# Mean of the values summed by TensorE, tokens four to a partition, GpSimd's bias rows earlier, late weights behind the first own rows

## The chip, the core and the metric

The kernel runs on one core of one Trainium2 chip. What is compared is the device time of a whole run in microseconds (us): the median of several runs of each kernel. Beside it stands one profiled execution, from which all rows below come.

## What is computed

The kernel is one layer of graph attention with a feed-forward part, with 2048 tokens, 256 features and 8 heads of 32. The adjacency `adj` is a 2048x2048 matrix of 0 and 1 with about one edge in 512, so some four edges per target row.

```python
hs = layer_norm(x, ln1_scale, ln1_bias) * mask;  ht = layer_norm(h_target, ...) * mask
q = (ht @ Wq + bq) / sqrt(32);  k = hs @ Wk + bk;  v = hs @ Wv + bv
logits = where(adj != 0, q . k, -1e30)            # per head
ctx = softmax(logits) @ v                         # a row without an edge gets the mean of v
ht = layer_norm(ht + ctx @ Wo + bo, ln2_scale, ln2_bias)
out = _layernorm(x + ht + gelu(ht @ W1) @ W2)
```

A target row with no edge has all logits at -1e30, so its softmax is flat and its context is the mean of all 2048 value rows. This mean is what the change computes in another way.

## The kernel before, in words

The kernel has two stages and a fallback path for dense graphs that these inputs do not take.

**Stage 1, the first 80 us.** The adjacency (16.8 MB of int32) is read in 16 tiles of 128 target rows (L559, `load_adj`). ScalarE turns each into a bf16 tile (`find_edges`, L1228). TensorE packs four rows at a time into integer keys (`make_keys`, L894 and L897), and VectorE picks the eight largest keys of each 128 columns (`pick_bank`, L1520), splits them into source number and bits (`split_keys`, L1526 to L1533), and lists each row's sources (`list_edges`, L1541 to L1547). This is done in four quarters. Interleaved with it, in an order written out by hand for every engine, the source tokens `x` are loaded in four chunks of 512 (`load_x`, L554), normed (VectorE `unit_stats` L1503 to L1509, GpSimd `rsqrt1` L665, ScalarE `normalise` L1211), turned (TensorE L871, ScalarE `copy_turned` L1219), projected to keys and values in 16 tiles (`project`, L883), and scaled by the node mask and biased by VectorE (`add_bias`, L1513) into `kv_out`. SyncE saves `kv_out` two tiles at a time to `kv_scratch` in DRAM (`save_kv`, L564), and copies `h_target` and `x` side by side into `tab_scratch` (L592). All these DMAs and all loads by SyncE share one hardware queue, q1; those that ScalarE issues are on q10, and GpSimd's gathers are on q0.

The values of all 16 tiles are added up by GpSimd (`add_v`, L679 and L681) into `v_total`, behind which TensorE makes the mean with one matmul over the partitions (`project_mean`, L907), ScalarE copies it out and saves it as row 0 of `kv_scratch` (L1269, L1271). GpSimd also makes three bf16 parts of the query and output biases (L737 to L747), after `add_v(1)` and behind the second quarter's split (`wait_listing(1)`). The node mask is loaded as 16 rows of 128 (L571), turned by TensorE (L915) and copied out by VectorE (L1558), and once more, per target, in the middle of the adjacency (L585).

At the end of stage 1 the rows are sorted by their number of edges. VectorE and TensorE compute every row's place (L1604 to L1658); `places` (L1656) is what the gathers need.

**Stage 2.** For each of 16 tiles of sorted rows GpSimd gathers the row's own tokens from `tab_scratch` (L765, "own rows") and, one edge slot at a time, keys and values from `kv_scratch` (L775). Before the first own gather it waits for `rows_copied`, before the first edge gather for all `kv_saved` and `mean_saved`. VectorE takes statistics (L1785), scores and weighs (L1689, L1691, L1730, L1736), ScalarE norms and applies gelu, TensorE projects (L976, L986), adds the attention's output (`project_out`, L995 to L1001, whose first call waits for all late weights), and runs the two feed-forward matmuls (L1023, L1032). GpSimd scatters the result (L801). `Wq` is loaded (L595) and scaled (L1876, by VectorE after the places), and then ln2's columns, `Wo`, `W1` and `W2` are loaded (L597, L601) as soon as the adjacency's buffers are free.

Every engine works in its written order, so an instruction that waits holds all that is behind it on that engine.

## Time and profile before

| | before |
|---|---|
| median of 3 runs | 292.06 us (291.75 to 292.36) |
| profiled execution | 291.37 us, of which the span (first to last instruction) is 289.6 us |
| TensorE busy | 223.8 us (77%) |
| VectorE busy | 212.3 us (73%) |
| ScalarE busy | 172.5 us (60%) |
| GpSimd busy | 185.2 us (64%) |
| bytes moved by DMA | 58.03 MB, mean 200 GB/s |

The profile names engines PE (TensorE), PEld (its weight loads), DVE (VectorE), ACT (ScalarE), POOL (GpSimd) and SP (SyncE); a q behind the name is the queue that issues. A row of the timeline gives the start, the busy time, the engine, the line and what is written and read; in brackets is how long the engine idled before it and what ended that. The chain of waits is followed back from the last instruction. The page's row of 40 slices gives tenths of busy time, one digit for each 7.24 us. `w_sb` in a row is `w1_sb` or `w2_sb`, which serve as adjacency buffers in stage 1.

### The profile page before, as it was taken

Reading aid. Unit: us, or ns where it says so; the run is one execution under the profiler, and the core shown is the slowest. Engines: PE = TensorE matmul, PEld = TensorE weight load, DVE = VectorE, ACT = ScalarE, POOL = GpSimd, SP = SyncE. Lnnn points to the kernel's source line nnn. Section 1 sums busy time; section 2 is a strip of 40 time slices with the busy share of each in tenths; the row PEclk is TensorE's granted clock in tenths of the full one; section 3 lists DMA queues with packets and bytes.
Section 4 is the critical chain, followed back from the end, with each engine's and each line's share of the span. In section 5 each row is a group of like instructions: output and inputs, shape, how many; then the busy total and the mean of one; then the engine's idle time right before and its main releaser. Section 6 shows DMA issues by size and latency. Waiting matters only on the chain.

```text
span 289.6 us, 4175 instructions
## 1 busy us (share of the span) xinstructions
PE 223.8 (77%) x1316; PEld 176.1 (61%) x1319; DVE 212.3 (73%) x614; ACT 172.5 (60%) x322; POOL 185.2 (64%) x205
## 2 busy tenths in 40 slices
PE   7397988841304876998889889997699899597990
PEld 7243443310202564997879768986589798496980
DVE  2444999999824875795977869899979988798111
ACT  2589999920504476776866798686376534353420
POOL 8581526981068768788887867888757687046542
PEclk9899999985555799999999999999979999999996
DMA  5999999999985536656555645556662455112120
GB/s 167 357 400 414 416 414 412 407 353 343 391 281 169 140 104 191 190 155 169 157 155 170 177 131 154 144 158 177 178 180 74 111 147 148 33 38 72 36 72 27
DMA packets 23457, 58.03 MB, mean 200 GB/s; under 512 B 4019, under 2 KB 12485, under 8 KB 21382
## 3 DMA queue, kind: packets, MB, share of 16 engines
q0 software_dynamic: 8368, 27.01, 32.5%
q1 hardware_dynamic: 14228, 29.91, 27.4%
q10 hardware_dynamic: 834, 0.79, 1.0%
q8 instruction: 12, 0.20, 0.3%
q14 instruction: 15, 0.12, 0.1%
HBM read 51.40 MB, written 10.49 MB: 214 GB/s over the span
## 4 chain that ended last, share of the span: by engine, by line
DVE 31%; POOL 25%; PE 16%; issue 9%; ACT 9%; DMA 8%; SPq 1%; POOLq 0%; ACTq 0%; DVEq 0%
POOL arena L775 16%; PE bank L1032 6%; ACT arena L1228 4%; PE score L1023 4%; DVE arena L1730 4%; POOL tab L765 4%; POOL rstd_late L795 4%; DMA tab<-in_x_dram 3%; DVE arena L1736 3%; DMA arena<-kv_scratch,places 3%; DVE cand L1520 2%; ACT tab L1211 2%; DVE logits L1691 2%; DVE arena L1689 2%; DMA tab<-tab_scratch,places 2%
## 5 line engine op out<-in xcount | busy, mean ns | idle before, releaser
L775 POOL DMA_INDIRECT arena<-kv_scratch,places x79 | 87.6, 1109 | 22.2 <-issue 22.2
L1023 PE MATMUL score<-h_t,w_sb 128*128 128x128 f32 x512 | 62.3, 275 | 0.0
L1032 PE MATMUL bank<-w_sb,gelu_t 128*128 128x256 f32 x256 | 61.8, 386 | 0.0
L1023 PEld LDWEIGHTS score<-h_t,w_sb 128*128 128x128 f32 x512 | 60.0, 192 | 0.6 <-ACT h_t L1363 0.3
L1032 PEld LDWEIGHTS bank<-w_sb,gelu_t 128*128 128x128 f32 x256 | 48.1, 195 | 5.9
L1309 ACT ACTIVATE gelu_t<-score 128x512 f32<-128x512 f32 x32 | 19.1, 597 | 26.6 <-PE score L1023 26.4
L795 POOL TENSOR_TENSOR rstd_late<-var_late,minus_half 128x1 f32<-128x1 f32 (+3 forms) x23 | 21.2, 922 | 20.9 <-DVE var_late L1799 20.6
L883 PE MATMUL bank<-tab,arena 128*128 128x512 f32 x64 | 30.2, 617 | 3.1 <-ACT arena L1219 1.8
L765 POOL DMA_INDIRECT tab<-tab_scratch,places x16 | 17.9, 1119 | 19.3 <-DVE place_value L1658 15.0
L1689 DVE TENSOR_TENSOR arena<-arena,query 128x1024 f32<-128x1024 f32 (+3 forms) x22 | 24.5, 1112 | 4.4 <-DMA arena<-kv_scratch,places 2.5
L1691 DVE TENSOR_REDUCE logits<-arena 128x32 f32<-128x1024 f32 (+3 forms) x22 | 24.4, 1110 | 0.8
L1730 DVE TENSOR_TENSOR arena<-arena,logits 128x1024 f32<-128x1024 f32 (+3 forms) x22 | 24.5, 1113 | 0.6
L883 PEld LDWEIGHTS bank<-tab,arena 128*128 128x128 f32 x64 | 11.9, 196 | 18.3 <-issue 16.1
L801 POOL DMA_INDIRECT out_dram<-tab,places x13 | 13.6, 1047 | 13.1 <-issue 11.6
L1010 PE MATMUL bank<-ident,h 128*128 128x128 f32 x32 | 7.0, 303 | 19.0 <-ACT h L1347 19.0
L1363 ACT ACTIVATE h_t<-bank,ln_col 128x128 f32<-128x128 f32 x32 | 12.9, 454 | 10.2 <-PE bank L1010 10.2
L986 PE MATMUL score<-wq_sb,own_t 128*128 128x256 f32 x64 | 18.2, 411 | 0.0
L1309 ACT ACT_TABLE_LOAD x14 | 18.0, 1283 | 0.2
L1010 PEld LDWEIGHTS bank<-ident,h 128*128 128x128 f32 x32 | 3.6, 144 | 23.6 <-ACT h L1347 23.2
L1736 DVE TENSOR_TENSOR arena<-arena 128x256 f32<-128x256 f32 (+1 forms) x32 | 17.1, 535 | 1.1
L1513 DVE SCALAR_TENSOR_TENSOR arena<-bank,node,tab 128x512 f32<-128x512 f32 x16 | 11.7, 740 | 8.2 <-PE bank L883 8.2
L1331 ACT ACTIVATE own_t<-score,ln_col 128x128 f32<-128x128 f32 x32 | 12.9, 454 | 7.4 <-PE score L976 7.4
(153 smaller groups left out, 425.7 us busy)
## 6 DMA issues: line engine op xcount, KB each, us to landing
arena<-in_adj_dram SPq DMA_DIRECT2D x6, 1024.0 KB, 12.0
w_sb<-in_adj_dram SPq DMA_DIRECT2D x6, 1024.0 KB, 13.1
kv_scratch<-arena SPq DMA_DIRECT2D x8, 512.0 KB, 10.4
tab<-in_x_dram SPq DMA_DIRECT2D x4, 512.0 KB, 11.3
own_t<-in_adj_dram SPq DMA_DIRECT2D x2, 1024.0 KB, 11.7
gelu_t<-in_adj_dram SPq DMA_DIRECT2D x2, 1024.0 KB, 10.9
tab_scratch<-in_L_gnn_h_target_dram SPq DMA_DIRECT2D x1, 2048.0 KB, 16.9
tab_scratch<-in_x_dram SPq DMA_DIRECT2D x1, 2048.0 KB, 20.7
```

Of the source, the lines that this page charges most:

```text
L765: pool.indirect_dma_start(tab[:, m % TR, :], None, tab_dram[:, :], at).then_inc(own_gathered[m % OWN_RING], 16)
L775: pool.indirect_dma_start(kv_ring[:, ring_at[m] + j, :], None, kv_dram[:, :], at).then_inc(gathered[m][piece], 16)
L795: pool.tensor_tensor(rstd_late[:, a:b], var_late[:, a:b], minus_half[:, 0:b - a], ALU.pow).then_inc(rstd_late_ready, 1)
L883: mm = pe.matmul(proj_ps[t % 2], h_t[:, t // CT % 2, k, t % CT * P:(t % CT + 1) * P], wkv[:, k, :], start=(k == 0), stop=(k == DK - 1))
L986: mm = pe.matmul(own_ps[:, D:KV], own_t[:, o % OWN_RING, k, :], wq_sb[:, k, :], start=False, stop=(k == DK - 1))
L1023: mm = pe.matmul(hid_ps[(2 * n + half) % 3][:, f % 4 * P:(f % 4 + 1) * P], w1_sb[:, k, f * P:(f + 1) * P], h2_t[:, n % 2, k, :], start=(k ...
L1032: pe.matmul(ff_ps[:, 0:D], gelu_t[:, n % 2, f, :], w2_sb[:, f, :], start=(f == 0), stop=False, skip_group_check=True)
L1309: act.activation(gelu_t[:, n % 2, 4 * half:4 * half + 4, :].rearrange("p a b -> p (a b)"), hid_ps[(2 * n + half) % 3], ACT.Gelu_apprx_tanh ...
L1689: dve.tensor_tensor(keys, keys, asked, ALU.mult).then_inc(score_step, 1)
L1691: dve.tensor_reduce(logits[:, r, a:b, :], keys.rearrange("p j (h d) -> p j h d", h=H), AX.X, ALU.add).then_inc(score_step, 1)
L1730: dve.tensor_tensor(by_head, by_head, part, ALU.mult).then_inc(weigh_step, 1)
L1736: dve.tensor_tensor(values[:, 0:half, :], values[:, 0:half, :], values[:, left - half:left, :], ALU.add).then_inc(weigh_step, 1)
```

## The change

- `project_mean` makes 16 matmuls, one per tile of `kv_out`, that accumulate in a bank (bank 0, not one of the key banks); GpSimd's `add_v`, its 16 operations and `v_total` go.
- Tokens lie four to a partition: token `4p + t` of a chunk is in partition p. Each partition's part of a `load_x` is then one run of 4 KB in DRAM, not four of 1 KB, and that of a `save_kv` one of 4 KB, not two of 2 KB. The node mask in this layout is the one per target, loaded once where the small one was (the early load is now 512 runs of 16 bytes); the turn on TensorE and the middle load go.
- GpSimd's bias parts wait for the first quarter's split instead of the second's.
- The last three saves of `kv_out` are issued by ScalarE: two behind `find_edges(15)`, one behind the counts of found edges. `Wq` is loaded behind the last adjacency tile, ahead of the saves, and scaled while VectorE waits for the places' matmuls.
- SyncE waits for the first own rows to land before it loads `Wo`, `W1` and `W2`.

```diff
             def load_x(c):
-                sp.dma_start(tok[:, c, :, :], x.rearrange("(c t p) d -> p c t d", p=P, t=CT)[:, c, :, :])...
+                sp.dma_start(tok[:, c, :, :], x.rearrange("(c p t) d -> p c t d", p=P, t=CT)[:, c, :, :])...
...
+        def save_kv(eng, t):
+            eng.wait_ge(kv_read, t + 2)
+            c, i = t // CT, t % CT
+            rows = kv_dram[1 + c * CH:1 + (c + 1) * CH, :].rearrange("(p i) n -> p i n", i=CT)
+            eng.dma_start(rows[:, i:i + 2, :], kv_out[:, t:t + 2, :]).then_inc(kv_saved, 16)
...
-            sp.dma_start(node_i[:, :], nodemask.rearrange("(t p) -> t p", p=P)).then_inc(node_loaded, 16)
+            sp.dma_start(node_target[:, :, :], nodemask.rearrange("(q u b) -> u q b", q=QUARTERS, b=UB),
+                         allow_slow_non_contiguous=True).then_inc(node_loaded, 16)
...
+            sp.dma_start(wq_sb[:, :, :], Wq.rearrange("(k p) n -> p k n", p=P)).then_inc(wq_loaded, 16)
             for t in range(0, TILES - 6, 2):
-                save_kv(t)
+                save_kv(sp, t)
             for w, a in enumerate((h_target, x)):
                 sp.dma_start(tab_dram[:, w * D:(w + 1) * D], a[:, :]).then_inc(rows_copied, 16)
-            for t in range(TILES - 6, TILES, 2):
-                save_kv(t)
-            sp.dma_start(wq_sb[:, :, :], Wq.rearrange("(k p) n -> p k n", p=P)).then_inc(wq_loaded, 16)
...
             wait_marked(sp, TILES - 1)
+            sp.wait_ge(own_gathered[0], 16)
             for dst, a in ((wo_sb, Wo), (w1_sb, W1), (w2_sb, W2)):
...
-            add_v(0)
-            wait_listing(0)
             pool.memset(below[:, :], 1.0).then_inc(const_step, 1)
...
-            add_v(1)
-            wait_listing(1)
             pool.memset(bias_rows[:, :], 0.0).then_inc(bias_step, 1)
             pool.wait_ge(bias_loaded, 32)
+            wait_listing(0)
...
-            add_v(2)
-            add_v(3)
...
             def project_mean():
                 pe.wait_ge(const_ready, 6)
-                pe.wait_ge(v_added, TILES)
-                pe.wait_ge(keys_read, QK * QUARTERS)
-                pe.matmul(mean_ps[0:CW, 0:D], mean_ones[:, :], v_total[:, :], start=True, stop=True)...
+                pe.wait_ge(h_copied, 2 * DK * CHUNKS)
+                for t in range(TILES):
+                    pe.wait_ge(kv_read, t + 1)
+                    mm = pe.matmul(mean_ps[0:CW, 0:D], mean_ones[:, :], kv_out[:, t, D:KV], start=(t == 0), stop=(t == TILES - 1))
...
             find_edges(15)
+            save_kv(act, TILES - 6)
+            save_kv(act, TILES - 4)
             for q in range(QUARTERS - 1):
...
+            save_kv(act, TILES - 2)
...
             unit_stats(0)
             dve.wait_ge(node_loaded, 16)
-            dve.tensor_scalar(node_rows[:, :], node_i[:, :], 1.0, None, ALU.is_equal).then_inc(node_ready, 1)
+            dve.tensor_scalar(node[:, :], node_target[:, :, :].rearrange("p q b -> p (q b)"), 1.0, None,
+                              ALU.is_equal).then_inc(node_ready, 1)
             unit_stats(1)
...
+            dve.wait_ge(wq_loaded, 16)
+            dve.tensor_scalar(wq_sb[:, :, :], wq_sb[:, :, :], Q_SCALE, None, ALU.mult).then_inc(node_ready, 1)
             dve.wait_ge(placed, 1)
```

## Rows read from the trace of the kernel before

**Rows 1.** The page's 40 slices: TensorE's granted clock and the DMA engines' busy share.
```profile
PEclk9899999985555799999999999999979999999996
DMA  5999999999985536656555645556662455112120
```

**Rows 2.** Chain of waits, in order of time: start us, us, what.
```profile
2.85 9.11 DMA tab<-in_x_dram
...
73.00 0.20 PE score L944
...
79.95 0.29 DVE places L1656
...
81.11 4.49 DMA tab<-tab_scratch,places
...
120.57 0.88 PE bank L1001 x4
```

**Rows 3.** Timeline of VectorE, first and last operation of splits 1, 2 and 3.
```profile
45.68 0.80 DVE L1526 CAST cand_i<-cand 128x128 int32<-128x128 f32 x1
...
48.39 0.69 DVE L1533 TENSOR_TENSOR arena<-arena,cand_source 128x512 f32<-128x512 int32 x1
...
56.86 0.21 DVE L1526 CAST cand_i<-cand 128x128 int32<-128x128 f32 x1
...
59.18 1.16 DVE L1533 TENSOR_TENSOR arena<-arena,cand_source 128x512 f32<-128x512 int32 x1
...
67.45 0.23 DVE L1526 CAST cand_i<-cand 128x128 int32<-128x128 f32 x1
...
68.51 0.69 DVE L1533 TENSOR_TENSOR arena<-arena,cand_source 128x512 f32<-128x512 int32 x1
```

**Rows 4.** Timeline of GpSimd: a sum of values, first and last bias operation, next sum.
```profile
45.68 3.99 POOL L679 TENSOR_TENSOR v_total<-v_total,arena 128x256 f32<-128x256 f32 x4
...
50.22 0.86 POOL L739 TENSOR_SCALAR h<-h 1x256 f32<-1x256 f32 x1
...
58.16 0.63 POOL L747 COPY bias_rows<-y_sum 1x512 bf16<-1x512 bf16 x1
59.06 3.60 POOL L679 TENSOR_TENSOR v_total<-v_total,arena 128x256 f32<-128x256 f32 x4 [0.27 <-POOL bias_rows L747]
```

**Rows 5.** Timeline of ScalarE: chunk 1's norm and the last adjacency tile.
```profile
15.56 2.07 ACT L1211 ACTIVATE tab<-tab,shift,rstd 128x256 f32<-128x256 f32 x4 [1.15 <-POOL shift L667]
...
55.26 1.93 ACT L1228 ACTIVATE arena<-arena 128x2048 bf16<-128x2048 int32 x1
```

**Rows 6.** DMA in 5 to 6, 43 to 44, 45 to 55 and 61 to 63 us.
```profile
DMA packets 332, 0.19 MB, mean 189 GB/s; under 512 B 148, under 2 KB 332, under 8 KB 332
...
DMA packets 231, 0.39 MB, mean 388 GB/s; under 512 B 184, under 2 KB 184, under 8 KB 184
...
DMA packets 841, 4.14 MB, mean 414 GB/s; under 512 B 74, under 2 KB 74, under 8 KB 423
...
DMA packets 709, 0.72 MB, mean 362 GB/s; under 512 B 2, under 2 KB 708, under 8 KB 709
```

**Rows 7.** DMA issues, KB, us to landing; started 1.8, 53.2, 69.5, 74.5, 85.1 us.
```profile
ln_col<-in_L_gnn_ln_bias_dram SPq DMA_DIRECT2D x1, 1.0 KB, 6.3
...
tab_scratch<-in_x_dram SPq DMA_DIRECT2D x1, 2048.0 KB, 20.7
...
kv_scratch<-arena SPq DMA_DIRECT2D x1, 512.0 KB, 8.2
...
w_sb<-in_L_gnn_W_dram SPq DMA_DIRECT2D x1, 1024.0 KB, 10.4
...
tab<-tab_scratch,places POOLq DMA_INDIRECT x1, 3.5
```

**Rows 8.** TensorE: the mean's two passes (durations in ns), and the first output projection.
```profile
L907 PE MATMUL score<-v_total,mean_ones x2: 603/617/631, 67.6 to 68.0; 128*32 128x256 f32 x2
...
97.45 0.27 PE L995 MATMUL bank<-bias_rows,ones_bf 128*128 128x256 bf16 x1
```

More of the change, by code:

```diff
@@ L304, in graph_attention @@
         const_ready = sem("const_ready")
-        node_turned = sem("node_turned")
+        natural_loaded = sem("natural_loaded")
+        natural_ready = sem("natural_ready")
         node_ready = sem("node_ready")
@@ L667, in rsqrt1 @@
                 pool.tensor_tensor(shift[:, c, :], minus_mean[:, c, :], rstd[:, c, :], ALU.mult).then_inc(rstd_ready, 1)
-            def add_v(c):
-                if c < QUARTERS - 1:
-                    pool.wait_ge(keys_read, QK * c + 1)
-                else:
-                    wait_listing(c - 1)
-                for t in range(CT * c, CT * (c + 1)):
-                    pool.wait_ge(kv_read, t + 1)
-                    if t > 0:
-                        pool.wait_ge(v_added, t)
-                        pool.tensor_tensor(v_total[:, :], v_total[:, :], kv_out[:, t, D:KV], ALU.add).then_inc(v_added, 1)
-                    else:
-                        pool.tensor_copy(v_total[:, :], kv_out[:, t, D:KV]).then_inc(v_added, 1)
             def wait_listing(q):
@@ L924, in _ @@
             turn_rows(2)
-            pe.wait_ge(node_ready, 2)
             make_keys(0)
```

43 lines of the change are left out of this document (16 added, 27 removed).

## The prediction

> **What bounds the kernel now.** I read the page's 40 slices first. DMA is at 9 tenths from slice 2 to slice 11, that is from 7 to 80 us, and mostly at 5 or 6 tenths later [rows 1]. So in stage 1 the DMA queue is as full as it can be (414 GB/s in a stretch of it [rows 6]), and every transfer that is added ahead of something needed delays that. Then the chain of waits, in order of time. It goes from the landing of chunk 1 of `x` (2.85 + 9.11 = 11.96) through ScalarE, then through VectorE to `places` at 79.95 (ready at 80.2), then from the first own gather, issued at 81.11 and landed at 85.60 [rows 2], through the pipeline of stage 2. In that stage GpSimd's gathers, VectorE and TensorE hand the chain to each other, and nothing in it depends on the clock time at which it began. So I take what the start of stage 2 gains or loses as the gain or loss of the whole, less what stage 2's own first steps lose.
>
> Two things must both be there for the first own gather: `places` and the copies in `tab_scratch`. In the kernel before, `places` is late (80.2) and the copies land at 53.2 + 20.7 = 73.9 [rows 7]. I work out both for the changed kernel.
>
> **Places: the splits of keys.** The timeline of VectorE shows the same seven operations three times. Split 3, with GpSimd idle, goes from 67.45 to 69.20: 1.75 us. Split 1 goes from 45.68 to 49.08, 3.40 us, and split 2 from 56.86 to 60.34, 3.48 us [rows 3]. In the timeline of GpSimd, split 1 lies beside a sum of values (45.68 to 49.67), split 2 beside the end of the bias parts (until 58.79) and the next sum (from 59.06) [rows 4]. Without the sums and with the bias parts elsewhere the splits cost 1.75 each: 1.65 + 1.73 = 3.4 us less. The bias parts take 50.22 to 58.79, 8.6 us [rows 4]; behind split 0, which ends at 37.4, they run until 46.0, over the first 0.3 of split 1. I take back 0.3. Behind the wait for split 0 GpSimd has only the bias parts and then the gathers, which wait for `places` anyway. VectorE is busy without a gap from 45 to 72, and what it waits for next comes in time, as I follow the written orders: `make_keys(2)` has its first bank at 50.5, when VectorE would come at 50.7, and the next ones 0.65 apart; the last adjacency tile is done at 57.2 [rows 5], so the last keys stand at 60.8 and the first bank of them at 58.8, when VectorE comes at 61. So places gains 3.1: 80.2 - 3.1 = 77.1.
>
> Scaling `Wq` (0.43 us) moves into the wait for the places' matmuls, an idle 0.90 us of VectorE, and costs nothing; `Wq` is loaded by 57. If that cover were gone it would cost 0.43.
>
> **The mean.** The 16 matmuls stand behind `make_keys(3)`, so they start at 60.8 (the value tiles are all ready at about 61). A two-pass matmul of 256 columns takes 0.22 x 2 = 0.43 us at the full clock (four passes in 0.88 [rows 2]), and 0.86 at the half clock (the old mean's passes start at 67.6 and 68.0 [rows 8]). 16 x 0.43 = 6.9 us, until 67.7. The classes' matmul behind it ran at 73.0 [rows 2] and is needed at 73.0 - 3.1 = 69.9. So the mean is free at the full clock, which slices 3 to 8 show (9 tenths) [rows 1], and TensorE goes from the keys straight on. Its save by ScalarE lands long before 77. The turn of the mask on TensorE that goes was not on the path.
>
> **The head: chunk 1 of x.** ScalarE waits 1.15 us for it before 15.56 and then works without a gap until 57.2 [rows 5], so a delay of chunk 1 delays all of stage 1, and at most 1.15 can be won. Two edits act on it. The node mask now is 512 runs of 16 bytes ahead of it, not 16 runs of 512. The two ln1 loads are such runs (512 of 4 bytes): the second lands at 1.83 + 6.3 = 8.1, with 148 small packets in a microsecond between [rows 6, 7]; at that rate 512 take 3.5 us. In the full queue the same mask load put 184 small packets into a microsecond while the rate fell only from 414 to 388 GB/s [rows 6]: four such microseconds cost 0.25 us. Against that, chunks 0 and 1 come in runs of 4 KB. Each took some 2 to 3 us for 0.52 MB, and at 414 GB/s it is 1.3: 0.8 to 2 for both. The sum is between 0.25 - 2.0 = -1.75 (of which 1.15 counts) and 3.5 - 0.8 = +2.7. I take +0.5, nearer to the ln1 loads, which stand in the same stretch.
> The Trainium skill (DMA: Bandwidth & Descriptors, "Why small descriptors are slow (HBM only)") puts the price of a small packet at some three cycles of an inner bus. By that, 32 packets for each of 16 engines would be an estimated 0.2 us, and the head would be a gain of about 1. The early row speaks against it and the row of the full queue for it.
>
> **The copies' landing.** Ahead of the end of the copies there are now: `Wq`, 0.26 MB, 0.65 us; and three saves of 0.52 MB, which used to be behind them and are now on ScalarE's queue from 57.3 and 61 on. At 414 GB/s 1.57 MB are 3.8 us if the queues only share, and less if the copies, which run at 362 GB/s or below [rows 6], leave room: from 0.9. I take 3.2. The mask load of the middle (0.25) goes, and the longer runs of x and of the saves save some 0.2. 73.9 + 0.65 + 3.2 - 0.45 + 0.5 of the head = 77.8; between 74 and 80.5. The issues and their waits for `kv_read` hold ScalarE in a stretch in which it waited for VectorE anyway; behind them are the counts of found edges, needed near 69.
>
> **The start of stage 2.** Places at 77.1 + 0.5 = 77.6, copies at 77.8. GpSimd issued the first gather 0.9 after places; 0.43 of that is beside the scaling of `Wq`, which is gone, and the copies come with an idle engine. The last save, which the first edge gather needs, landed at 69.5 + 8.2 = 77.7 [rows 7] and lands earlier now. I take 0.5: issue at 78.3 instead of 81.1, 2.8 earlier. The gather then took 4.49 under the tail of `W2` (landing at 74.5 + 10.4 = 84.9) and takes 3.5 with the queue free [rows 2, 7]. So own row 0 lands at 81.8 instead of 85.6: 3.8.
>
> **What the late weights give back.** They start at 81.8 now; behind that wait SyncE has nothing else that is used. 2.36 MB beside gathers of 0.26 MB each 1.3 us (200 GB/s) have some 214 of 414 GB/s: 11 us and a landing of 1.5, 94.3. The first output projection ran at 97.45 [rows 8] and would be wanted at 93.7: 0.6 late. The gathers of rows 1 and 2 take up to 1.0 longer (4.49 against 3.5); VectorE waits for both, but little of it is on the path: 0.3. Together 0.9, between 0 and 4. The rest of stage 2 is not touched; 0.2 for a pipeline that doesn't shift as one.
>
> Sum: -3.8 + 0.9 + 0.2 = -2.7. On the profiled execution, 291.37 - 2.7 = 288.7. The median of the runs is 0.7 above that execution, so 292.06 - 2.7 = **289.4 us**.
>
> **Rivals.** *More of it comes.* Small packets cost little and the two queues fill each other: head -1.0, copies at 74.5, places at 76.1, weights in time: about -4.9, 287.2. For it: the row of the full queue. 0.16.
> *The mask's small packets hold chunk 1.* Head +2.2: places 79.3, copies 79.5, gather at 80.0: -1.1, less 1.0 for the faster landing, plus 0.9 and 0.2: -1.0, 291.1. 0.14.
> *The weights become the wait.* If the engines take turns packet by packet, the gathers' 2 KB against the 1 KB of `Wo` and `W2` leave those a third, 138 GB/s: 1.31 MB in 9.5 us and `W1` in 4 more, landed at 96.8, 3.1 late instead of 0.6: 291.9. 0.08.
> The Trainium skill (the same page, "Queues, rings and completion order") says that an engine goes round its queues packet by packet. The trace shows only that the first gather was a microsecond longer beside the weights.
> *The splits don't get shorter*, because GpSimd is not what stretches them: places at 80.7, landing 84.7: about -0.5 + 0.2, 291.8. The match in three cases speaks against it. 0.05.
> *Slower: the mean at the half clock.* If TensorE's clock falls behind the keys, where the kernel before had 8 tenths in slice 9 and 5 in slice 10, with no matmul from 61.5 to 67.6 [rows 1, 8], the mean takes 13.8 us, until 74.6, and the classes' matmul waits 4.7 beyond 69.9: 289.4 + 4.7 = 294.1. It decides from (69.9 - 60.8)/16 = 0.57 us per tile. Against it: TensorE has no gap between keys and mean. 0.09, a blocked issue of ScalarE's saves among it.
>
> **How the numbers follow.** My forecast has the remaining 0.48. A difference of 0.2% (0.6 us) is about what can be told from none. Faster by more (below 291.5): forecast, more of it, most of the mask's case: 0.76. Within: part of the mask's, the weights' and the splits' cases, 0.12. Slower: the half clock and the ends of the mask's and the weights' case, 0.12. The range is 287.0 to 292.4: it leaves out half of the good case and the slower one.
>
> **What the profile would show.** Splits 1 and 2 at about 1.8 us; 32 passes of the mean in 7 us at granted clock 1.0, ended before `in_class`; chunk 1's statistics start at 12.5; first own gather issued at 78 to 79 and landed in 3.5; `Wo`, `W1`, `W2` landed by 94 and no idle before the first output projection beyond 1 us. The prediction is wrong if the gather waits for the copies beyond 80, if chunk 1 lands after 14, or if stage 2 takes longer from the first landing to the end than the 204 us (289.6 - 85.6) it took.

## The result, and the profile of the changed kernel

The changed kernel is slower. The first measurement, on the chip of the profiles shown here, gave 297.03 us (median of 4; 295.69 to 297.58) against 292.21 for the kernel before: a ratio of 1.0136 (95% interval 1.0074 to 1.0198; the quotient of the two medians alone is 1.0165). A second one on another chip, with more runs, gave 1.0052 (1.0016 to 1.0089). So it is slower by half a per cent to 1.4%; why the two chips differ isn't shown. The ratios compare executions in the faster of the chip's two states only, and the traces of a_spsaves and b_pace below, which are of slower executions, are read only for the start of stage 2. Forecast was 289.4, or 0.991. The profiled execution took 295.69 us (span 293.8); that of the kernel before took 291.37, so the two traces differ by +4.3 where the sum said -2.7.

The page's slices (to set beside [rows 1]) already show two things: a hole in the DMA engines' work at 73 to 81 us (slice 11, 5 tenths where it was 9), and TensorE's granted clock at 5 tenths in slices 11 to 14, where it was in slices 10 to 13 before, so that it rises a slice later, with a 7 in slice 17, at 118 us, where it was 9.

```profile
PEclk9899999997555599799999999999979999979998
DMA  6999999999579526645565645455652445101010
```

Stage 1 went as forecast, or better. The timeline of VectorE, with the first and last operations of splits 1 and 2 and then `places` (line numbers are those of the changed kernel):

```profile
45.07 0.58 DVE L1506 CAST cand_i<-cand 128x128 int32<-128x128 f32 x1
...
46.50 0.69 DVE L1513 TENSOR_TENSOR arena<-arena,cand_source 128x512 f32<-128x512 int32 x1
...
54.96 0.22 DVE L1506 CAST cand_i<-cand 128x128 int32<-128x128 f32 x1
...
56.02 0.69 DVE L1513 TENSOR_TENSOR arena<-arena,cand_source 128x512 f32<-128x512 int32 x1
...
76.33 0.27 DVE L1637 TENSOR_SCALAR places<-score 128x111 uint32<-128x111 f32 x1 [0.57 <-PE score L932]
```

Split 1 takes 2.1 us (45.07 to 47.19) instead of 3.4, split 2 1.75 instead of 3.48 [rows 3], and `places` starts at 76.33 instead of 79.95 [rows 2]. Then the start of stage 2: GpSimd's first own gather, and on VectorE the statistics of own rows 0, 1 and 2, which start when their gathers have landed.

```profile
79.53 1.23 POOL L743 DMA_INDIRECT tab<-tab_scratch,places  x1 [33.95 <-DMA tab_scratch<-in_x_dram]
```
```profile
83.28 0.43 DVE L1766 BATCH_NORM_STATS2 stats_own<-tab 128x6 f32<-128x256 f32 x1 [6.31 <-DMA tab<-tab_scratch,places]
...
90.71 0.43 DVE L1766 BATCH_NORM_STATS2 stats_own<-tab 128x6 f32<-128x256 f32 x1 [5.36 <-DMA tab<-tab_scratch,places]
...
93.09 0.43 DVE L1766 BATCH_NORM_STATS2 stats_own<-tab 128x6 f32<-128x256 f32 x1 [0.70 <-DMA tab<-tab_scratch,places]
```

The gather waits for the copy of `x` and not for `places`. Where the copies are in time the first gather is issued 0.57 behind the start of `places` (a_spsaves and a_paced below), which would be 76.9 here: 2.6 us are waited away, and 1.6 are left of the lead. It lands after 3.7 us, 2.35 earlier than before. Own row 1, issued at 83.56, takes 7.1, and own row 2, issued at 85.33, takes 7.7. In the kernel before the same three statistics start at 85.62, 88.67 and 90.74, behind gathers of 4.5, 3.5 and 3.4 us:

```profile
85.62 0.43 DVE L1785 BATCH_NORM_STATS2 stats_own<-tab 128x6 f32<-128x256 f32 x1 [4.58 <-DMA tab<-tab_scratch,places]
...
88.67 0.43 DVE L1785 BATCH_NORM_STATS2 stats_own<-tab 128x6 f32<-128x256 f32 x1 [1.36 <-DMA tab<-tab_scratch,places]
...
90.74 0.43 DVE L1785 BATCH_NORM_STATS2 stats_own<-tab 128x6 f32<-128x256 f32 x1 [0.36 <-DMA tab<-tab_scratch,places]
```

So a lead of 2.35 at row 0 has become a lag of 2.35 at row 2: 4.7 us given back in two gathers. The chain of waits of the changed kernel goes through both losses, the copy of `x` and the gather of own row 2:

```profile
49.28 29.35 DMA tab_scratch<-in_x_dram
...
85.33 7.73 DMA tab<-tab_scratch,places
93.09 0.44 DVE stats_own L1766
```

What the DMA engines did meanwhile, by queue, in 86 to 88, 88 to 90 and 90 to 92 us (columns: packets, MB, share of the engines' time; q0 is GpSimd's queue with the gathers, q1 SyncE's with the weights):

```profile
q1 hardware_dynamic: 299, 0.66, 94.6%
q0 software_dynamic: 19, 0.05, 5.8%
...
q1 hardware_dynamic: 155, 0.50, 62.1%
q0 software_dynamic: 81, 0.29, 38.7%
...
q0 software_dynamic: 145, 0.46, 56.6%
q1 hardware_dynamic: 281, 0.33, 45.8%
```

So the gathers get almost nothing for two microseconds and about half of the engines' time in the four behind; in 84 to 94 us together their queue moved 1.07 MB and the weights' 2.27.

The further way of the lag is best seen at one operation that comes once per target tile, the turn of `h2` on TensorE (tiles 0, 1 and 2). Kernel before, then the changed one:

```profile
102.84 0.44 PE L1010 MATMUL bank<-ident,h 128*128 128x128 f32 x2 [1.36 <-ACT h L1347]
...
115.85 0.44 PE L1010 MATMUL bank<-ident,h 128*128 128x128 f32 x2 [2.55 <-ACT h L1347]
...
125.98 0.38 PE L1010 MATMUL bank<-ident,h 128*128 128x128 f32 x2
```
```profile
106.03 0.44 PE L987 MATMUL bank<-ident,h 128*128 128x128 f32 x2 [1.35 <-ACT h L1327]
...
118.11 0.69 PE L987 MATMUL bank<-ident,h 128*128 128x128 f32 x2 [2.57 <-ACT h L1327]
...
129.79 0.38 PE L987 MATMUL bank<-ident,h 128*128 128x128 f32 x2
```

The lag is 3.2 at tile 0, 2.3 at tile 1, 3.8 at tile 2, and then it stays between 3.6 and 3.8 for eleven tiles and ends at 4.5 on the last two: stage 2 shifts as one, except at a few tiles. The step from tile 1 to 2 takes 11.7 us here and 10.1 before. The windows of 116 to 120 us show why (columns: busy time of PE, PEld, DVE, ACT, POOL with counts, granted clock, DMA share, GB/s):

```profile
116.00:118.00 2.00, 0.00 (x0) 0.00 (x0) 0.16 (x1) 0.51 (x1) 1.80 (x3) 0.98 0.71 174
118.00:120.00 2.00, 1.89 (x6) 1.63 (x7) 1.91 (x3) 1.20 (x4) 1.49 (x2) 0.50 0.58 184
```

TensorE has nothing to do for 2.5 us, the granted clock falls to 0.50, the lower of its two levels (1.2 of 2.4 GHz), and the next eight matmuls take 3.24 us instead of 1.89. The kernel before has the same hole at 114 to 116 us, where its clock stayed at 1.00. From tile 9 to 10 both kernels have a fall: 11.8 us with the clock at 0.50 and 0.65 in 210 to 214 us before, 11.7 with 0.50 and 0.78 in 214 to 218 in the changed kernel, where a_pace_only, a_warm and others below take 10.1. And the last step of the lag, from 3.8 to 4.5, is one of the changed kernel alone: its clock is at 0.50 and 0.68 in 258 to 262 us, where that of the kernel before stays at 1.00.

### The profile page after: what moved, and what is told of

Read it like the earlier page. It is cut to its first block, busy times and chain, and to the rows that moved or that the text cites. A ratio compares the mean times of both kernels' runs of the same rounds, so it can differ in the third digit from the quotient of the medians.

```text
span 293.8 us, 4205 instructions
## 1 busy us (share of the span) xinstructions
PE 234.7 (80%) x1348; PEld 183.2 (62%) x1348; DVE 210.7 (72%) x613; ACT 172.5 (59%) x322; POOL 172.8 (59%) x189
## 4 chain that ended last, share of the span: by engine, by line
POOL 26%; DMA 18%; PE 17%; DVE 16%; ACT 10%; issue 9%; SPq 2%; POOLq 0%; ACTq 0%
POOL arena L753 16%; DMA tab_scratch<-in_x_dram 10%; PE bank L1009 7%; ACT arena L1205 6%; PE score L1000 5%; POOL tab L743 4%; POOL rstd_late L773 4%; DVE arena L1711 3%; DMA arena<-kv_scratch,places 3%; DMA node_target<-in_nodemask_dram 3%; DMA tab<-tab_scratch,places 3%; DVE arena L1717 2%; ACT tab L1188 2%; PE bank L978 2%; ACT arena L1196 2%
## 5 line engine op out<-in xcount | busy, mean ns | idle before, releaser
L1009 PE MATMUL bank<-w_sb,gelu_t 128*128 128x256 f32 x256 | 63.8, 396 | 0.0
L1000 PEld LDWEIGHTS score<-h_t,w_sb 128*128 128x128 f32 x512 | 60.7, 194 | 0.6 <-ACT h_t L1343 0.3
L1009 PEld LDWEIGHTS bank<-w_sb,gelu_t 128*128 128x128 f32 x256 | 49.5, 200 | 6.3
L963 PE MATMUL score<-wq_sb,own_t 128*128 128x256 f32 x64 | 19.1, 428 | 0.0
L1296 ACT ACTIVATE tab<-tab,shift_late,rstd_late 128x256 f32<-128x256 f32 x16 | 9.4, 598 | 16.1 <-DVE shift_late L1810 16.1
L953 PE MATMUL score<-ident,tab 128*128 128x128 f32 x32 | 7.0, 305 | 14.5 <-ACT tab L1296 9.8
L1493 DVE SCALAR_TENSOR_TENSOR arena<-bank,node,tab 128x512 f32<-128x512 f32 x16 | 11.7, 743 | 8.6 <-PE bank L860 8.6
## 6 DMA issues: line engine op xcount, KB each, us to landing
tab_scratch<-in_x_dram SPq DMA_DIRECT2D x1, 2048.0 KB, 29.4
```

Of the source, the lines that this page charges most:

```text
L963: mm = pe.matmul(own_ps[:, D:KV], own_t[:, o % OWN_RING, k, :], wq_sb[:, k, :], start=False, stop=(k == DK - 1))
L1000: mm = pe.matmul(hid_ps[(2 * n + half) % 3][:, f % 4 * P:(f % 4 + 1) * P], w1_sb[:, k, f * P:(f + 1) * P], h2_t[:, n % 2, k, :], start=(k ...
L1009: pe.matmul(ff_ps[:, 0:D], gelu_t[:, n % 2, f, :], w2_sb[:, f, :], start=(f == 0), stop=False, skip_group_check=True)
```

## The experiments

Every ratio is to runs of the kernel before on the same chip. a_nowait, a_spsaves, a_both, b_wait, b_pace and a_burst2 ran on a slower chip (298.0 instead of 292.8 us for the kernel before); a_both has only four runs, from 292.4 to 300.4 us. The last column has the starts of VectorE's statistics of own rows 0, 1 and 2. All times in it are of one execution of each kernel.

| kernel | ratio (95% interval) | copies landed | first gather issued | own rows 0, 1, 2 |
|---|---|---|---|---|
| before | 1 | 73.9 | 81.11 | 85.6, 88.7, 90.7 |
| changed | 1.0136 (1.0074 to 1.0198) | 78.6 | 79.53 | 83.3, 90.7, 93.1 |
| after2, the same again | 1.0052 (1.0016 to 1.0089) | 79.6 | 80.5 | 84.2, 91.9, 93.5 |
| a_nowait | 1.0036 (0.9992 to 1.0081) | 79.8 | 80.7 | 86.8, 88.5, 91.9 |
| a_spsaves | 0.9934 (0.9887 to 0.9982) | 73.5 | 77.0 | 80.8, 88.6, 90.2 |
| a_both | 0.9878 (0.9785 to 0.9971) | 74.9 | 78.0 | 83.9, 87.3, 88.9 |
| b_wait | 1.0111 (1.0070 to 1.0152) | 74.9 | 81.3 | 85.0, 92.6, 94.4 |
| b_mean | 0.9978 (0.9944 to 1.0011) | 74.0 | 77.5 | 83.9, 87.5, 89.1 |
| b_layout | 0.9973 (0.9938 to 1.0007) | 73.3 | 78.9 | 84.5, 86.6, 89.6 |
| b_actsaves | 0.9998 (0.9964 to 1.0031) | 77.8 | 79.8 | 85.7, 87.6, 90.7 |
| a_paced | 0.9888 (0.9843 to 0.9932) | 73.6 | 76.9 | 80.7, 84.6, 86.2 |
| a_pace_only | 0.9914 (0.9876 to 0.9952) | 78.7 | 79.6 | 83.3, 87.3, 88.9 |
| a_warmhole | 0.9882 (0.9837 to 0.9927) | 73.9 | 77.9 | 81.6, 85.5, 87.1 |
| a_warm | 0.9833 (0.9783 to 0.9883) | 74.6 | 78.0 | 81.8, 85.7, 87.4 |
| b_pace | 0.9981 (0.9937 to 1.0025) | 74.5 | 81.0 | 84.7, 88.8, 90.4 |
| a_burst2 | 1.0148 (1.0082 to 1.0214) | 79.9 | 80.8 | 84.5, 88.6, 90.2 |

### The wait and ScalarE's saves, undone one by one

Theory at this point: the wait ahead of the late weights puts them beside the gathers of own rows 1 and 2 (cause 1), and the saves on ScalarE's queue make the copies land late (cause 2). a_nowait undoes the first, a_spsaves the second, a_both both; b_wait adds the wait to the kernel before.

```diff
 # a_nowait
-            sp.wait_ge(own_gathered[0], 16)
 # a_spsaves: behind the copies, on SyncE
+            for t in range(TILES - 6, TILES, 2):
+                save_kv(sp, t)
 # and on ScalarE
-            save_kv(act, TILES - 6)
-            save_kv(act, TILES - 4)
...
-            save_kv(act, TILES - 2)
```

> The changed kernel with SyncE's wait for the first own rows taken out: Wo, W1 and W2 follow ln2's columns at once, as in the kernel before. Theory 1 (the late weights' wait costs): the weights no longer start at 83.3 on the queue beside the gathers of own rows 1 and 2, which took 7.1 and 7.7 us; they start as the copies end, at 78, and are through at about 85. Own rows 1 and 2 then take 3.5 to 4.5, own row 0 up to 5; the median falls from 297.0 to about 293 to 294. Theory 2 (only the saves on ScalarE's queue, which slow the copies, cost): the copies still land at 78.6, and nothing is won: 296 to 297.

> The changed kernel with the last three saves back on SyncE's queue behind the copies. Theory 2 (the saves beside the copies make these land late): copies at 73.9 + 0.65 (Wq) = 74 to 75.5 instead of 78.6, first own gather issued at 77 when places is ready, 2.4 earlier; the first edge gather waits for the saves until 78 to 79. Theory 1 adds that rows 1 and 2 still take over 7 us. Both together: 294.5. If the copies still land at 78, neither the queue nor the order is what slows them, but the new layout of the saves or of x.

> Both edits: no wait ahead of the late weights, and the last three saves on SyncE's queue. What is left of the change is the mean by TensorE, the bias parts earlier, the layout and Wq's place. Theories 1 and 2 together: first own gather at 77, the weights' data until 85 beside the first gathers, 290.5 to 292. If it is 294 or more, a part of the change that neither theory names costs the time.

> The kernel before with one added line: SyncE waits for the first own rows before it loads Wo, W1 and W2. Theory 1: own row 0 lands in 3.5 instead of 4.5, then rows 1 and 2 take over 7 us instead of 3.5, and the total is 3 to 5 us above before: 295 to 297. If theory 1 is wrong, 291.5 to 292.5.

The wait by itself costs the kernel before 1.1% (b_wait), inside the 295 to 297 expected of 292, and its trace shows the same picture: own row 0 in 3.7 us, rows 1 and 2 in 7.3 and 7.4.

```profile
92.62 0.43 DVE L1786 BATCH_NORM_STATS2 stats_own<-tab 128x6 f32<-128x256 f32 x1 [5.58 <-DMA tab<-tab_scratch,places]
...
94.43 0.43 DVE L1786 BATCH_NORM_STATS2 stats_own<-tab 128x6 f32<-128x256 f32 x1
```

(VectorE in b_wait, own rows 1 and 2.) With the saves back on SyncE's queue, taking the wait away brings another half per cent at the centre (0.9934 to 0.9878), though these two intervals overlap. But a_nowait, with the saves still on ScalarE's queue, stands at 1.0036. As a ratio to the kernel before that is what was expected (293 to 294 of 292.2), but beside the 1.0052 of the changed kernel's second measurement it is no gain that can be told. Without the wait the weights leave at 75 to 77 us, the copies land at 79.8, and the first gather falls right into the weights and takes 6.1 us. So taking away the wait alone is not half of the mend: while the copies are late, both places for the weights, ahead of the first gather and behind it, collide with a gather.

```profile
86.79 0.43 DVE L1765 BATCH_NORM_STATS2 stats_own<-tab 128x6 f32<-128x256 f32 x1 [9.56 <-DMA tab<-tab_scratch,places]
...
91.88 0.43 DVE L1765 BATCH_NORM_STATS2 stats_own<-tab 128x6 f32<-128x256 f32 x1 [0.34 <-DMA tab<-tab_scratch,places]
```

(VectorE in a_nowait, own rows 0 and 2.) In a_spsaves the first gather is issued at 77.0, right behind `places`, as the copies have landed at 73.5; rows 1 and 2 then take 7.5 and 7.3. All three are 2.1 to 2.9 earlier than in the changed kernel, and 0.9934 is the larger of the two single steps: by these ratios the copies' landing counts more than the wait while the weights are a burst. a_spsaves and a_both both stand better than expected (294.5, and 290.5 to 292, of 292.2).

### The changed kernel again, and its gaining parts on the kernel before

after2 is the changed kernel itself. b_mean is the kernel before with the mean by TensorE and the bias parts behind the first split, and b_layout the kernel before with tokens four to a partition and the one load of the node mask; neither has the wait or the moved saves.

```diff
 # b_mean
-            add_v(0)
-            wait_listing(0)
...
+            wait_listing(0)
...
+                for t in range(TILES):
+                    pe.wait_ge(kv_read, t + 1)
+                    mm = pe.matmul(mean_ps[0:CW, 0:D], mean_ones[:, :], kv_out[:, t, D:KV], start=(t == 0), stop=(t == TILES - 1))
 # b_layout
-                sp.dma_start(tok[:, c, :, :], x.rearrange("(c t p) d -> p c t d", p=P, t=CT)[:, c, :, :]).then_inc(x_loaded[c], 16)
+                sp.dma_start(tok[:, c, :, :], x.rearrange("(c p t) d -> p c t d", p=P, t=CT)[:, c, :, :]).then_inc(x_loaded[c], 16)
```

> The changed kernel again, beside the three others on one chip. It should stand at 1.010 to 1.018 of before. With the four runs before it gives a two by two table of the wait ahead of the weights and of the saves on ScalarE's queue.

> The kernel before with only the mean by TensorE and GpSimd's bias parts behind the first split; layout, node mask, saves, Wq and late weights as before. Theory A (the sums of values stretched VectorE's splits): splits 1 and 2 take 1.8 to 2.1 us, places is ready at 77 instead of 80, and no DMA is moved. The first gathers then start under the last of the copies' successors and the late weights, which end at 85: own row 0 takes 5 to 7 us, so of the 3 us some 1 to 2 arrive: 0.993 to 0.997 of before. Theory B (places alone decides): 0.989. If neither: 1.00.

> The kernel before with only tokens four to a partition: runs of 4 KB for x and for the saves, one load of the node mask in 512 small runs at the start, no turn of it, no load in the middle. Queues and order as before. If the layout is harmless (chunk 1's statistics at 11.5 as in the changed kernel): 0.996 to 1.000, with the copies landed at 73 to 74. If it is the layout that makes the copies land late (77 or later), the time is the same or up to 0.3% more.

after2, at 1.0052, stands below the 1.010 to 1.018 expected. Its trace has the same losses (own rows 1 and 2 take 7.3 and 7.2 us), and the first turn of `h2` is at 106.55; its step from tile 1 to 2 takes 10.1.

Both parts do what they say, and neither alone can be told from no change. b_mean has `places` 3.0 earlier (forecast for this part: 3.1) and issues the first gather 3.6 earlier, but that gather then lies in the weights of 74 to 84 us and takes 6.3 us, and own row 2 comes 1.6 earlier. b_layout's `places` are 2.3 earlier: 0.6 from the head (ScalarE's norm of chunk 1 at 14.97 instead of 15.56), the rest from split 1, beside which GpSimd's sum happened to be over. So about half of each gain in `places` is eaten by the weights' burst, which in the kernel before stands where the first gather now comes. The rest is lost later, at tiles where TensorE's clock differs. b_mean keeps 1.4 to 1.8 us at every turn of `h2` down to the last but one; the step to the last takes 10.6 us, where the kernel before takes 8.9, with the clock at 0.78, 0.50 and 0.86 in 262 to 268 us and at 1.00 before. b_layout's first output projection starts at 96.42, 1.0 earlier than before, but its clock stays at 0.50 until 100 and at 0.51 until 102 us, where the kernel before has 0.66 in 96 to 98 and 1.00 behind it, and its first turn of `h2` is 0.8 later.

```profile
83.87 0.43 DVE L1766 BATCH_NORM_STATS2 stats_own<-tab 128x6 f32<-128x256 f32 x1 [4.61 <-DMA tab<-tab_scratch,places]
```

### The weights paced

If the burst is what costs, five transfers of 0.26 to 0.52 MB, each behind the landing of the one before, should cost little. a_paced has also the saves on SyncE's queue, a_pace_only has not.

```diff
-            sp.wait_ge(own_gathered[0], 16)
-            for dst, a in ((wo_sb, Wo), (w1_sb, W1), (w2_sb, W2)):
-                sp.dma_start(dst[:, :, :], a.rearrange("(k p) n -> p k n", p=P)).then_inc(late_loaded, 16)
+            sp.wait_ge(own_gathered[1], 16)
+            sp.dma_start(wo_sb[:, :, :], Wo.rearrange("(k p) n -> p k n", p=P)).then_inc(late_loaded, 16)
+            sp.wait_ge(late_loaded, 48)
+            for h in range(2):
+                sp.dma_start(w1_sb[:, h, :], W1[h * P:(h + 1) * P, :]).then_inc(late_loaded, 16)
+                sp.wait_ge(late_loaded, 16 * (4 + h))
+            for h in range(2):
+                sp.dma_start(w2_sb[:, FK // 2 * h:FK // 2 * (h + 1), :],
+                             W2.rearrange("(k p) n -> p k n", p=P)[:, FK // 2 * h:FK // 2 * (h + 1), :]).then_inc(late_loaded, 16)
+                sp.wait_ge(late_loaded, 16 * (6 + h))
```

TensorE waits for each piece where it first uses it.

> The changed kernel with the three saves back on SyncE's queue, and the late weights in five pieces: Wo behind own row 1, then two halves of W1 and two of W2, each behind the landing of the piece before, with TensorE waiting for each only where it is used. Theory 1 (a burst of weights starves the gathers): own rows 1 and 2 take 4 to 5 us instead of over 7, own row 2 has landed by 87.5 instead of 93, no wait at the first output projection: 0.980 to 0.986 of before, the fastest of all. If the gathers still take 7 us, it is not the burst but any transfer beside them.

> The changed kernel with the late weights in five pieces, each behind the landing of the one before and the first behind own row 1 instead of own row 0; the last three saves stay on ScalarE's queue. Theory: the two losses add up. The copies still land near 79, so the first own gather is issued at 79.5 to 80.5 and lands 3.7 later at 83.5 to 84; gathers of own rows 1 and 2 take 3.4 to 3.8 and not 7.1 to 7.7; the first statistics of a residual come near 98.5 to 99 (95.96 in the kernel that has both mends, 101.8 to 102.7 in the changed kernel). Total 0.992 to 0.998 of before. Rival: the pace matters only where the first gather is early, and the total is that of the changed kernel, 1.005 or more.

```profile
80.71 0.43 DVE L1773 BATCH_NORM_STATS2 stats_own<-tab 128x6 f32<-128x256 f32 x1 [3.72 <-DMA tab<-tab_scratch,places]
...
84.59 0.43 DVE L1773 BATCH_NORM_STATS2 stats_own<-tab 128x6 f32<-128x256 f32 x1 [1.84 <-DMA tab<-tab_scratch,places]
...
86.20 0.42 DVE L1773 BATCH_NORM_STATS2 stats_own<-tab 128x6 f32<-128x256 f32 x1
```

a_paced: all three gathers take 3.5 to 3.8 us, own row 2 comes 4.5 earlier than before and 6.9 earlier than in the changed kernel, and the kernel is 1.1% faster than before: less than the 1.4 to 2.0% expected. a_pace_only, which differs from the changed kernel in nothing but the weights, stands at 0.9914, better than the 0.992 to 0.998 expected: pacing is worth 1.4% there (1.0052 against 0.9914, each against the kernel before on its own chip, with intervals that don't meet; against the first measurement it is 2.2%). Its gathers of own rows 1 and 2 are issued at 83.63 and 85.41, within 0.1 of the changed kernel's, and take 3.7 and 3.5 us. The saves on ScalarE's queue are 0.3% on top at the centre, within the intervals and between two chips. a_paced stands no better than a_both (0.9878, with a wide interval), which has the weights in one burst ahead of the gathers; so that pacing beats undoing both edits isn't shown.

### Is it the place of the weights, or the pace, and does the kernel before gain too?

```diff
 # b_pace: the kernel before, with the paced weights above
 # a_burst2: the changed kernel, one burst, later
-            sp.wait_ge(own_gathered[0], 16)
+            sp.wait_ge(own_gathered[2], 16)
```

> The kernel before with one edit alone: the late weights in five pieces, each behind the landing of the one before and the first behind own row 1's gather (in the kernel before they are issued in one burst at 74 to 75 and land by 84.9). It tells whether the gain of the mended kernels (0.989 and 0.991 of before) is a gain of the changed kernel's other parts or one of the pace alone. Theory (the pace saves what the burst costs, and the other parts bring 2 to 3 us by themselves): here the first own gather is issued at 81 as before and takes 3.5 to 3.8 instead of 4.5, own rows 1 and 2 land no earlier than before less 0.5, first turn of h2 within 1 us of 102.84; total 0.997 to 1.001. Rival (the pace is the whole gain, and the other parts bring nothing): total 0.991 or less.

> The changed kernel with the wait for own row 0 ahead of the late weights replaced by one for own row 2, so that the same three weights leave in one burst of 2.36 MB behind own row 2's landing at about 87.5 instead of own row 0's at 83.3. It tells place from pace. Theory (the burst takes the DMA engines from whatever gather comes next): own rows 1 and 2 take 3.4 to 3.8; the gathers issued at 87 to 90 (edges of the first tiles and own row 3) take 7 or more; the weights land at 98 to 100 and the first output projection waits for them, as W1 and W2 are needed with Wo by the same wait; first turn of h2 at 102.5 to 105; total 0.999 to 1.006. Rival (only the own rows 1 and 2 matter): first turn of h2 at 101 to 102 and total 0.990 to 0.995, as with the paced weights.

b_pace is at 0.9981: the pace alone brings the kernel before nothing that can be told. Its `places` at 80 come behind the worst of the burst, and pacing only frees the last microsecond of it. The theory holds: pace and the earlier `places` bring 1% together and next to nothing singly. a_burst2 is the slowest of all, 1.0148, beyond its expected 1.006, though its interval overlaps with that of the changed kernel's first measurement. Its own rows are in time (row 2 at 90.2), and then the burst meets what comes next:

```profile
98.96 0.43 DVE L1766 BATCH_NORM_STATS2 stats_own<-tab 128x6 f32<-128x256 f32 x1 [2.62 <-DMA tab<-tab_scratch,places]
```

This is own row 3, whose gather was issued at 91.59: 7.4 us again. But it is not what makes this kernel slow. The second wait that the expectation named, TensorE's for the weights, is the one on the path:

```profile
103.12 0.40 PE L972 MATMUL bank<-bias_rows,ones_bf 128*128 128x256 bf16 x1 [6.26 <-DMA w_sb<-in_L_gnn_W_dram]
```

The first output projection waits 6.26 us for the last weights. Without that wait it would have come near 96.9, 0.6 earlier than before (97.45), as own row 2 came 0.5 earlier; with it the first turn of `h2` is at 109.5, against 102.8. The chain of waits says the same: it holds 11.97 us of the weights' transfer from 91.10 on, and not own row 3. So this run shows that the gather beside a burst doubles in another place too, but its total is the price of weights that land too late, and not of that gather.

### ScalarE's saves alone

```diff
 # the kernel before, with the last three saves on ScalarE's queue
-            for t in range(TILES - 6, TILES, 2):
-                save_kv(t)
...
+            save_kv(act, TILES - 6)
+            save_kv(act, TILES - 4)
...
+            save_kv(act, TILES - 2)
```

> The kernel before with one part of the change alone: the last three saves of keys and values (0.52 MB each) are issued from ScalarE's queue, behind its last conversion of adjacency, instead of from SyncE's queue behind the copies. In the kernel before the copies landed at 73.9 and the first own gather was issued at 81.1, so there is room of 7 us. Theory A (bytes on a second queue hold the copies back): the copies are issued no later and land 5 us later, at 78 to 80, which places at 80 still hide: the first own gather is issued at 81 and the total is within 0.3% of before (1.000). Theory B (the late landing in the changed kernel came from its longer runs or its order, not from ScalarE's saves): the copies land at 73 to 75 here too. If the saves on ScalarE's queue cost ScalarE something later, the total rises by 0.3% or more and the first own gather is not later.

```profile
tab_scratch<-in_x_dram SPq DMA_DIRECT2D x1, 2048.0 KB, 24.6
```

Theory A held: the copy of `x`, issued at 53.19 as before, lands after 24.6 us instead of 20.7 [rows 7], at 77.8, 3.9 later, and `places` hide it. Total 0.9998. In this trace `places` start at 78.65, 1.3 earlier than before, and why isn't shown; the first gather, issued at 79.8 and not at 81, takes 5.8 us beside the weights, and own row 0 comes at 85.7 as before. The changed kernel's copy of `x` starts 3.9 earlier than that (49.28) and takes 29.4 us. Part of the rest lies ahead of it in the queue. Part is the rate: in 57 to 74 us all queues of b_actsaves moved 6.25 MB, and those of the changed kernel 5.30 MB.

```profile
DMA packets 4900, 6.25 MB, mean 368 GB/s; under 512 B 107, under 2 KB 3592, under 8 KB 4899
q1 hardware_dynamic: 4083, 4.67, 82.9%
q10 hardware_dynamic: 816, 1.57, 24.5%
```
```profile
DMA packets 3641, 5.30 MB, mean 312 GB/s; under 512 B 92, under 2 KB 3103, under 8 KB 3639
q1 hardware_dynamic: 3205, 3.70, 77.4%
q10 hardware_dynamic: 434, 1.58, 29.0%
```

(First b_actsaves, then the changed kernel; q10 is ScalarE's queue.) The saves are the same 1.57 MB; with tokens four to a partition they go in 434 packets instead of 816, and beside them SyncE's queue moves less. The kernel before had 356 GB/s in these microseconds, with SyncE's queue alone. The longer runs, entered in the sum as a gain of 0.2, go with a loss here; that they are its cause no run isolates. On SyncE's queue alone they do no harm to the landing: in b_layout, with 347 GB/s in the same 17 us, the copies land at 73.3, 0.6 earlier than before.

### TensorE's clock

In a_paced 3.7 us were won at tile 1 and 2.2 at tile 2. Idle transposes (128 columns, into a bank's unused columns) were put into the hole (a_warmhole), and into that and every gap from the mean to the first turn of `h2` (a_warm).

```diff
+                    if first:
+                        pe.wait_ge(h2_copied, DK)
+                        for _ in range(14):
+                            pe.transpose(banks[2][:, CH - P:CH], ident[:, :], ident[:, :])
                     if s + 1 < hi:
                         turn_h2(s + 1)
 # a_warm, as well: 12 behind the mean, 18 ahead of the places' matmuls, 34 behind, 4, 2 and 6 later
```

> The mended kernel (paced weights, saves on SyncE's queue; 0.9888 of before) with 14 idle transposes of 128 columns for TensorE put in front of the turn of the second tile of h2, where TensorE had nothing to do for 2.5 us (109.7 to 112.2) and the granted clock then fell to 0.5 between 112 and 115. In the traces the second to third tile took 11.7 us after such a fall and 10.1 where the clock stayed. Theory (the start's gain is partly given back because TensorE's clock falls in a hole): the clock stays at 1.0 there, the third tile comes 1.5 us earlier against the second, total 0.984 to 0.987 of before. Rival: the fall comes from what was before the hole or the 1.5 us are given back further down, total unchanged at 0.988 to 0.990; or the transposes hold the turn up and it is slower by up to 0.3%.

> As the kernel with the idle transposes in the hole, and in addition idle transposes of 128 columns in every gap of TensorE from the mean of the values to the first turn of h2: 12 behind the mean, 18 ahead of the matmuls of the places, 34 behind them, 4 and 2 between the first own rows' steps, 6 ahead of the first turn of h2. Theory (the half clock between 71 and 98 costs time in the start of stage 2): the granted clock stays at 0.9 to 1.0 from 66 to 110, the query projections take 1.0 instead of 1.9 and the first output projection 1.0 instead of 2.07, h2's first turn comes 1 to 2 us earlier than 100.16, total 0.980 to 0.985. Rival: the clock falls in spite of them, the 34 transposes then take 11 us instead of 6 and hold up the first own turn by up to 4: total 0.99 to 1.00.

The windows of 110 to 114 us, a_paced and then a_warmhole:

```profile
110.00:112.00 2.00, 0.00 (x0) 0.00 (x0) 0.26 (x2) 1.70 (x4) 1.80 (x3) 0.98 0.75 180
112.00:114.00 2.00, 1.83 (x6) 1.56 (x7) 1.93 (x3) 1.20 (x4) 1.47 (x2) 0.50 0.56 174
```
```profile
110.00:112.00 2.00, 2.00 (x16) 1.85 (x15) 0.57 (x4) 1.93 (x3) 1.69 (x2) 1.00 0.75 227
112.00:114.00 2.00, 1.66 (x12) 1.32 (x11) 1.52 (x3) 1.25 (x3) 1.53 (x2) 1.00 0.58 154
```

The clock stays up and the step from tile 1 to 2 takes 10.1 us instead of 11.7, but tile 1 itself comes 0.7 later (112.84 against 112.17), so 0.9 is left in the trace, and the ratio, 0.9882, is that of a_paced. The transposes were not in tile 1's way: they end at 112.50, and the turn waits 0.34 more for ScalarE's `h`; why that came later isn't shown. In a_warm the granted clock of the whole kernel is 0.943 to 0.963 in its runs, against 0.917 to 0.930 in those of a_paced; yet the first turn of `h2`, at 100.36, is no earlier than the 100.16 of a_paced. Its 0.9833 is the fastest of all, and its interval overlaps with that of a_paced.

That the half clock costs something of the gain is likely by the tiles' steps and by the stretch ahead of the first turn of `h2`. From the first output projection to that turn the kernel before takes 5.4 us with the clock risen at 97, and b_mean and b_actsaves take 5.3 and 5.35; the changed kernel takes 7.0 with the clock at 0.50 until 104, and a_paced 7.2: of the 4.5 us that it leads at the projection (92.99 against 97.45) 2.7 are left at the turn. a_warm, with the clock at 1.00 from 94 to 100, takes 6.7 all the same; there TensorE waits 2.01 us for ScalarE's query, after a gather of own row 3 that took 6.0 us. And a_paced loses 1.7 once more on its last tile (clock at 0.77, 0.50 and 0.87 in 261 to 267). How much of the total it is, these runs don't settle.

## Why the prediction was wrong, point by point

- **Splits and bias parts: right.** 3.4 less, minus 0.3 for the bias parts' end, was forecast; `places` came 3.6 earlier. Of this 0.6 is the head, whose sign was wrong: it was forecast 0.5 later and came 0.6 earlier (chunk 1's norm on ScalarE starts at 14.96 instead of 15.56 [rows 5], after waiting 0.65 instead of 1.15). The 512 small packets of the mask cost less than the early row suggested, and the row of the full queue was the better one.
- **The mean on TensorE: right.** 32 passes in 7.07 us at the full clock, from 59.51, off the path. The slower rival built on it had nothing to it.
- **The copies: right in kind, at the late end.** 78.6 against 77.8 forecast and 80.5 as bound. The term for the saves was 3.2; b_actsaves measured 3.9 with the old runs. The head hid more: with its -0.6 for the +0.5 the sum would have been 76.7, so the copies' own terms were 1.9 short, 0.7 of it in the saves and the rest with the lower rate of all queues, whose cause is open. The first gather came at 79.53 and not 78.3, and own row 0 2.35 earlier instead of 3.8. This costs 1.4 of the gain.
- **What the late weights give back: this step failed.** "The gathers of rows 1 and 2 take up to 1.0 longer ... 0.3" was sized by the one gather that ran in the tail of `W2` [rows 2], 4.49 us. Full in the burst they take 7.1 and 7.7 us. 2.35 ahead at row 0 are 2.35 behind at row 2: 4.7 us given back, where 0.9 was the term and 4 its bound. The reasoning shared 414 GB/s between two queues by their need. The trace shows 0.66 MB for the weights and 0.05 MB for the gathers in 86 to 88 us, and about half of the engines' time for each in the next four. b_wait shows the same doubling and 1.1% from this one edit, and a_pace_only, with the same gathers issued at the same times beside paced weights, has neither. And "VectorE waits for both, but little of it is on the path" was wrong too: in the table the total goes with own row 2, the later the slower, from 0.983 to 0.989 at 86 to 87 us to 1.005 to 1.014 at 93 to 94. The one clear exception is a_burst2, whose loss is the wait for the weights behind own row 2. The chain of waits has own row 2 in it, too.
- **The queue rule.** The rival "the weights become the wait" had 0.08 and put their landing at 96.8. They landed at 96.7, and cost nothing there: the first output projection follows at 99.05 without a wait. Its mechanism was looked for in the wrong transfer; as a wait for the weights it came true in a_burst2 alone. The Trainium skill (DMA: Bandwidth & Descriptors, "Queues, rings and completion order") has an engine go round its queues packet by packet, where a packet is several descriptors and need not be what the profile counts as one. By that each of two busy queues would get every second turn. The trace agrees with it in a part of the burst: in 90 to 92 us the gathers' queue has 145 packets of 426 and 57% of the engines' time. In 86 to 88 us it has 19 against the weights' 299, and in 92 to 94 us 14 against 673, while the gather of own row 2 was on its way until 93.1. There the measurement decides; why the share changes so isn't shown by these runs.
- **"0.2 for a pipeline that doesn't shift as one": too small.** It does shift as one, but a hole of TensorE may or may not pull the clock down; the fall at tile 2 is 1.6 us, the one in 258 to 262 is 0.7, as TensorE waits less behind it. From own row 2's lag of 2.35 the trace goes to 1.6 at the first output projection (99.05 against 97.45) and to 3.2 at the first turn of `h2` (TensorE's clock is at half until 104, before it was until 97), then to 3.8 at tile 2 and 4.5 at the end. The premise was that nothing in stage 2 depends on the time at which it began; at these tiles, where TensorE's granted clock differs between the two traces, it didn't hold. The stated condition, that stage 2 takes longer from the first landing to the end than 204 us, is the one that came true: 210.5.

The sum with measured terms: -2.35 at own row 0, +4.7 in the gathers of rows 1 and 2, +0.9 until the first turn of `h2`, +0.6 up to tile 2 (a fall of 1.6, less 0.9 that the step before it won back), and +0.7 in the fall ahead of the last but one: +4.5, against 4.3 between the two executions. The +0.9 until the first turn is 1.6 behind the projection less 0.7 ahead of it; that the clock is its cause is argued from the two traces and not isolated.

## What to carry to other kernels

When a wait moves bulk loads, ask which small, latency-bound transfers they will now lie beside, and price those by the worst beside a full burst, not by one at its edge; here each gather doubled, from about 3.6 to 7.5 us. Send bulk loads that have time in pieces behind each other's landing: that made 1.4% here, and let most of an earlier `places` come through. And look at when they are needed: the burst moved two rows further made TensorE wait 6.3 us for it. An edit that gains nothing alone (b_mean, b_layout, b_pace) may be one half of a gain: look at what took its microseconds in the trace before it is dropped.

## What the hardware showed that was not expected

- A gather of 128 rows of 2 KB takes 3.4 to 3.8 us with the queues free or, for own rows 0 to 2, with a paced load near it, 4.5 to 6.3 in a burst's tail and 7.1 to 7.7 full in it, the last in five traces of four kernels (the changed one in two, b_wait, a_spsaves, and own row 3 of a_burst2). Own row 3 of a_warm took 6.0 us beside a paced piece of `W1`.
- Saves on a second queue left the rate of all queues at 368 GB/s in packets of 2 KB (356 without them), and it was 312 and 320 in the two traces of the changed kernel, where they go in half as many packets.
- The granted clock fell in a hole of 2.5 us of TensorE in one execution (the changed kernel, tile 1) and not in another of nearly the same program (the kernel before, b_actsaves); such a fall cost 0.7 to 1.7 us, up to half a per cent of this kernel, as much as several of the edits studied here.
